# Layer 1's attention: the row scores in one PSUM bank and four parts, the output projection in a bank of its own

## What is computed

```python
def _L1_xattn_ref(values, keys, query, Wv, Wk, Wq, Wo, bo):
    ...                                     # 16 heads of 16 numbers each
    v = jnp.einsum('nlhd,ed->nlhe', v, Wv)
    k = jnp.einsum('nlhd,ed->nlhe', k, Wk)
    q = jnp.einsum('nlhd,ed->nlhe', q, Wq)
    energy = jnp.einsum('nqhd,nkhd->nhqk', q, k)
    attention = jax.nn.softmax(energy / jnp.sqrt(jnp.float32(EMBED)), axis=-1)
    out = jnp.einsum('nhql,nlhd->nqhd', attention, v).reshape(N, Lq, EMBED)
    return out @ Wo.T + bo
...
x = x + _L1_xattn_ref(ctx_1024, ctx_1024, _layernorm(x, axis=-1), ...)
```

## Time and profile before

| what | value |
|---|---|
| median of 3 runs (lowest, highest) | 1107.93 us (1105.76, 1111.91) |
| the profiled execution: its own time, its span | 1103.02 us, 1101.2 us |
| mean granted TensorE clock, of full speed | 0.921 |
| PE busy | 918.6 us, 83% of the span |
| DVE busy | 640.5 us, 58% |
| ACT busy | 490.3 us, 45% |
| POOL busy | 417.8 us, 38% |

### The profile page before, as it was taken

One profiled execution on the slowest core, in us unless ns is written; L12 is line 12 of the kernel. 1 busy time (PEld: TensorE's weight loads), 2 busy tenths in 40 slices (PEclk: granted clock), 3 DMA queues, 4 the chain that ended last, 5 costly groups with the idle time before them and its releaser, 6 DMA issues. The chain is left out here.

```text
span 1101.2 us, 24348 instructions
## 1 busy us (share of the span) xinstructions
PE 918.6 (83%) x8038; PEld 630.3 (57%) x8038; DVE 640.5 (58%) x1554; ACT 490.3 (45%) x832; POOL 417.8 (38%) x560
## 2 busy tenths in 40 slices
PE   6789999997412999999999999997378888877996
PEld 4445555553202888889888988875124444443552
DVE  4556777774697444545444444443698888435561
ACT  1487777775222333333333333322055555634653
POOL 2476776761100334242312222110875553004440
PEclk9799999998655999999999999999589999996998
DMA  6332434331523111111112121111632221000122
GB/s 178 65 105 61 118 97 122 94 105 61 176 83 115 35 54 45 54 47 51 53 45 58 40 58 40 49 31 32 172 92 73 71 66 34 1 1 1 47 51 58
DMA packets 76289, 75.45 MB, mean 69 GB/s; under 512 B 25290, under 2 KB 69434, under 8 KB 76186
## 3 DMA queue, kind: packets, MB, share of 16 engines
q1 hardware_dynamic: 69706, 56.31, 17.6%
q0 software_dynamic: 6480, 17.70, 6.1%
HBM read 51.64 MB, written 22.34 MB: 67 GB/s over the span
## 5 line engine op out<-in xcount | busy, mean ns | idle before, releaser
L1327 DVE CAST hh_e<-h_e 128x512 f16<-128x512 f32 (+1 forms) x156 | 66.7, 427 | 213.2 <-ACT h_e L1303 123.4
L1253 PE MATMUL up_ps<-xT_e,experts 128*128 128x256 f16 (+1 forms) x624 | 165.1, 266 | 4.8 <-ACT h_e L1303 3.2
L1255 PE MATMUL up_ps<-xT_e,experts 128*128 128x256 f16 (+1 forms) x624 | 165.1, 265 | 0.0
L1254 PE MATMUL up_ps<-xT_e,experts 128*128 128x256 f16 (+1 forms) x624 | 164.3, 264 | 0.0
L1267 PE MATMUL y_ps<-experts,hh_e 128*128 x568 | 155.1, 273 | 1.2 <-DVE hh_e L1329 0.3
L1268 PE MATMUL y_ps<-experts,hh_e 128*128 x568 | 155.1, 273 | 0.0
L1269 PE MATMUL y_ps<-experts,hh_e 128*128 x568 | 154.9, 273 | 0.0
L1188 POOL COPY idx_e<-token 128x2 int32 (+2 forms) x39 | 22.5, 577 | 304.6 <-PE xT_ps_e L1233 249.6
L1303 ACT ACTIVATE h_e<-up_ps 128x512 f32<-128x512 f32 (+1 forms) x156 | 87.2, 559 | 109.1 <-PE up_ps L1255 109.1
L1329 DVE TENSOR_TENSOR hh_e<-h_e,hh_e 128x512 f16<-128x512 f32 (+1 forms) x156 | 100.6, 645 | 5.4
L1537 ACT ACTIVATE prob_a<-sT_ps_a 77x1024 f32<-77x1024 f32 x64 | 64.8, 1014 | 50.4 <-PE sT_ps_a L1467 50.4
(11 more groups left out here) (275 smaller groups left out, 1938.0 us busy)
## 6 DMA issues: line engine op xcount, KB each, us to landing
experts<-in_L_ffn_w SPq DMA_DIRECT2D x22, 512.0 KB, 4.1
y_scratch<-y_e SPq DMA_DIRECT2D x32, 256.0 KB, 3.0
w_r<-in_L_ffn_w SPq DMA_DIRECT2D x10, 512.0 KB, 3.8
x<-in_x SPq DMA_DIRECT2D x32, 128.0 KB, 4.1
experts<-in_x SPq DMA_DIRECT2D x64, 64.0 KB, 2.4
x_scratch<-experts SPq DMA_DIRECT2D x16, 256.0 KB, 2.5
xh_scratch<-experts SPq DMA_DIRECT2D x16, 256.0 KB, 2.7
x_a<-x_scratch SPq DMA_DIRECT2D x32, 128.0 KB, 2.1
```

What stands on the lines that cost most here:

```text
L1253: mm(out, w[0], xT[0][:, c, 0:W_], start=c == 0, stop=False)
L1254: mm(out, w[0], xT[1][:, c, 0:W_], start=False, stop=False)
L1255: last = mm(out, w[1], xT[0][:, c, 0:W_], start=False, stop=c == DC - 1)
L1327: nc.vector.tensor_copy(hh[0][own], h[own]).then_inc(hhi_ok, 1)
```

## The change

Two PSUM banks change their use. pair_ps is given up: t_ps and pr_ps each get a bank of their own, and s_ps shrinks from two banks to one. The four score parts are issued one at a time, spread over the step, and each waits for the maxima of the part just ahead of it. The maxima are spread over DVE's list in the same manner. rows_transposed waits for oT_ok (ACT has copied this step's heads out of t_ps) in place of x3_ok; the wait for x3_ok moves from heads_transposed to projection. No instruction of computation is added or taken away.

```diff
-        pair_ps, v_ps = L.bank("pair_ps_a"), L.bank("v_ps_a")
+        t_bank, pr_bank, v_ps, s_ps = (L.bank(f"{n}_ps_a") for n in ("t", "pr", "v", "s"))
...
-        t_ps, pr_ps = pair_ps[:, 0:D], pair_ps[:, D:2 * D]
-        s_ps = ctx.enter_context(nc.psum_tensor("s_ps_a", [P, 2, 512], F32))
+        t_ps, pr_ps = t_bank[:, 0:D], pr_bank[:, 0:D]
...
-                def scores(f, c):
+                def scores(f, i):
+
                     b = f // TB
-                    if c == 0:
+                    if i == 0:
                         pe.wait_ge(hi_ok, f + 1)
-                    for i in range(2):
-                        after(pe, max_ok, 4 * f + 2 * c + i - 1)
-                        mm(s_ps[:, i, 0:CH], xhi[:, f // 4 % 3, c, flat(f % 4, P)],
-                           G["khi"][1][:, b, ds((8 * c + 4 * i) * KEYS, CH)], start=True, stop=True).then_inc(s_done, 1)
+                    after(pe, max_ok, 4 * f + i)
+                    mm(s_ps[:, 0:CH], xhi[:, f // 4 % 3, i // 2, flat(f % 4, P)],
+                       G["khi"][1][:, b, ds(4 * i * KEYS, CH)], start=True, stop=True).then_inc(s_done, 1)
...
                 def heads_transposed(n):
                     pe.wait_ge(o_ok, n + 1)
                     pe.wait_ge(lo_ok, min(n + 11, NT))
-                    after(pe, x3_ok, n)
...
                 def projection(n):
                     pe.wait_ge(oT_ok, n + 1)
+                    after(pe, x3_ok, n)
...
                 def rows_transposed(f):
                     pe.wait_ge(xh_ok, f + 1)
                     after(pe, lo_ok, f)
-                    after(pe, x3_ok, min(f - 10, NT))
+                    after(pe, oT_ok, min(f - 10, NT))
...
                         scores(f, 0)
                     if 0 <= k < QUARTERS:
                         scores_by_key(k)
+                    if tile(f):
+                        scores(f, 1)
                     if tile(n):
                         heads_transposed(n)
                     if 0 <= k - 1 < QUARTERS:
                         values(k - 1)
                     if tile(f):
-                        scores(f, 1)
+                        scores(f, 2)
                     if tile(n):
                         projection(n)
                     if tile(f + 1):
                         rows_transposed(f + 1)
+                    if tile(f):
+                        scores(f, 3)
...
-                def maximum(f, c):
-                    for i in range(2):
-                        dve.wait_ge(s_done, 4 * f + 2 * c + i + 1)
...
+                def maximum(f, i):
+                    dve.wait_ge(s_done, 4 * f + i + 1)
...
                         maximum(f, 0)
                     if tile(f + 1):
                         normed_rows(f + 1)
+                    if tile(f):
+                        maximum(f, 1)
                     if tile(f + 2):
                         rows(f + 2)
+                    if tile(f):
+                        maximum(f, 2)
                     if tile(n):
                         result(n)
                     if tile(f):
-                        maximum(f, 1)
+                        maximum(f, 3)
```

More of the change, by code:

```diff
@@ L1601, in low @@
                                             ALU.subtract).then_inc(lo_ok, 1)
-                def maximum(f, c):
-                    for i in range(2):
-                        dve.wait_ge(s_done, 4 * f + 2 * c + i + 1)
-                        nc.vector.tensor_reduce(nmax[:, f // 4 % 2, f % 4, c, flat(i, 4)],
-                                                s_ps[:, i, 0:CH].rearrange("p (j k) -> p j k", j=4),
-                                                AX.X, ALU.max, negate=True).then_inc(max_ok, 1)
+                def maximum(f, i):
+                    dve.wait_ge(s_done, 4 * f + i + 1)
+                    nc.vector.tensor_reduce(nmax[:, f // 4 % 2, f % 4, i // 2, flat(i % 2, 4)],
+                                            s_ps[:, 0:CH].rearrange("p (j k) -> p j k", j=4),
+                                            AX.X, ALU.max, negate=True).then_inc(max_ok, 1)
                 def maxima(g):
```

## The result

| | median of the runs (lowest, highest) | runs |
|---|---|---|
| before | 1108.53 us (1105.76, 1111.91) | 6 |
| after | 1114.86 us (1113.18, 1116.92) | 6 |

The ratio after to before is 1.0052, with a 95% interval of 1.0032 to 1.0072: the change makes the kernel 6.3 us slower. The prediction said 1113.8 us, slower by 5.9.

A forecast was written before the change was run, and what follows sets the result against it. DVE was taken to bound rows alone, a chain between DVE, PE and ACT rows and quarters, one ring's waits the steady steps. Terms 5.7 + 5.1 - 5.2 + 0.3 = +5.9 us on 1107.93 gave 1113.8 us; range 1108 to 1119.

The forecast's parts named there:

- steps 0 to 4: Five steps with rows and quarters: a ring through PE's list makes 27.15 us against 22.05, +5.1; bounds +1 and +10.
- the base of before: Starting time: the profiled execution's 1103.02 us lies 4.9 below the median, so the forecast adds to 1107.93 us.
- Rows alone: First five tiles, DVE-bound: single-bank stalls before maxima 1, 3 and 0 add 5.7 us; bounds nothing and 6.4.
- 6.35 + 4 x 5.2 = 27.15: Rows-and-quarters regime: first step 6.35 us at the low clock, the other four 5.2 each at full clock.
- rival 1: Clock stays low longer in the rows-and-quarters steps: +1.2 for one more, +5 for all four; 1115 to 1119 us; chance 0.15.
- Steps with all three: Steady 21 tiles: ordinary step 5.22 us against 5.51, sum 115.6 against 120.81, -5.2; bounds 0 and -11.
- the ring: Steady step's last waits: projection, result, new rows' transposes, ACT's copy, DVE's low; PE idles 0.61 for result.
- The end: Step 26: heads_out of the next tile now stands behind scores 3, costing 0.3 us.
- Rival 2: Steady steps don't gain, from longer handoffs or stalls adding up in PE's list: +11, 1119 us; chance 0.12.
- Rival 3: Early steps cheaper: early terms +5 to +8, total 0 to +3, 1108 to 1111 us; chance 0.18.
- Rival 4: Faster: POOL's gathers pace the early regime, stalls fall in slack; -5 to -6, 1102 to 1103 us; chance 0.05.

The follow-up runs named there:

- lend_10: Kernel after, with odd score parts of tiles 0 to 9 in the projection's idle bank: 1103.64 us, ratio 0.9942 to before.
- filler: Kernel after plus useless 512-column matmuls in PE's gaps in steps -5 to 4: 1107.08 us, ratio 0.9977 to before.
- after_again: The kernel after, unchanged, run and profiled once more: 1114.9 us, ratio 1.0042 to before.
- before_filler: Kernel before plus four useless matmuls in each step with rows alone (steps -5 to -1): 1108.61 us, ratio 0.9991 to before.
- pairs: Kernel after's banks, but score parts and maxima in pairs again and result behind the last maximum: 1158.57 us, one execution.
- order_only: Kernel after's spread order of score parts and maxima, on the banks and waits of before: 1117.04 us, ratio 1.0077 to before.
- the second execution: The kernel before, unchanged, profiled once more: that execution took 1112.43 us where the first had 1103.02.
- split: lend_10 with rows divided in two on DVE's list, so xa stands in front of maximum 1: 1096.16 us, ratio 0.9912 to before.
- lend_filler: lend_10 plus four useless matmuls in each step with rows alone (steps -5 to -1): 1103.13 us, ratio 0.9941 to before.

## Why the prediction was right

The median lies 1.1 us above the forecast; the sign was right, and two terms of the sum were right by their steps. The term of steps 0 to 4 left out most of the low clock, and the base of before hid that.

*Rows alone*: +5.7 expected, +5.5 and +5.4 measured. The expected stalls were 0.295, 0.615 and 0.375 before maxima 1, 3 and 0; the idle times are 0.21, 0.53 and 0.27, and idle time counts from the end of the instruction ahead, which overlaps the next by some 0.08. lend_10 takes them away by a second bank and gets 5.0 back.

*Steps 0 to 4*: +5.1 expected, +10.3 and +8.9 measured against the profile that the prediction had. The first is just above the upper bound of +10. The failed step is the sum "6.35 + 4 x 5.2 = 27.15", which let one of five steps be at the low clock. The full-clock price was 0.2 a step too small (filler, 26.99 against 26.0). The steps of the kernel after took 6.59, 6.60, 6.53, 6.00 and 6.64, with a clock of 0.72 in the third, 0.54 in the fourth and 0.50 in the others; in after_again 6.46, 6.60, 6.53, 5.97 and 5.37, with 0.76, 0.50, 0.73, 0.71 and 0.93. This is rival 1's mechanism at its price of about +5, given a chance of 0.15. Between executions of the nearest clocks the term comes out at 4.6 to 4.9, so the banks' part of it was about right. The cause of the low clock is shown only so far that more matmuls in these steps raise it; the same code of before was itself granted 0.91, 0.83 and 0.73. lend_10 has its second bank in these steps too and still took 28.11 us at 0.70, 6 us more than the first execution of before and 1.7 more than before_filler at 0.73: most of that goes with the clock, and why it falls there is open.

*Steps with all three*: 115.6 us expected, 116.32 and 116.88 measured; the steps 5.22, 5.55, 6.12 and 5.0 are 5.27, 5.49, 6.17 and 4.87, and the first is 5.79 and 6.33, before the clock is up. The argument for a gain, that spread parts cover most of the round trip and that result leaves the ring, holds: pairs (1.55 a step without the spreading) and order_only (8.3 or 5.6 lost without the split bank) show that both are needed. The Trainium skill's rule of rotating banks (Perfetto Trace Analysis, Matmuls) speaks rightly in the first regime (5.0 us back in lend_10). In this one the change breaks it for the score parts and follows it for the transposes and the projection, which now have a bank each, and the second weighs more.

*The end*: +0.3 expected. From low(31) to the last result it took 43.2 us in both executions of before and 42.9 in both of after, so it is -0.3.

*The base.* The prediction moved its profiled time to the median by adding 4.9 to the whole, as if what the other executions take more lay where the change doesn't reach. Of the 9.4 us between the two profiled executions of before, 4.2 lie ahead of the attention, but 2.9 in its steps 0 to 4 and 2.7 in its steady part; before_filler, with the same steady code, has 26.38 and 124.15. There the change takes more away: the steady part gains 7.2 and 6.6 against the second execution, where 5.2 was expected, and steps 0 to 4 lose 7.4 and 6.0. Against the first execution nothing cancels, and the sum is 11.3. That the medians differ by 6.3 and 5.9 therefore rests on how a typical execution of before behaves in a ring without slack, which the prediction didn't know of. To that extent the closeness of the number was luck; the median alone would have passed for a full confirmation.

Rival 2 is out, as the steady part gains. Rival 3 is out, as the early steps cost more and not less. Rival 4 is out: POOL is busy 17.50 of 26.23 us, and DVE's idle time ends with PE's scores.

## What to carry to other kernels

A PSUM bank that is written anew after each read costs a round trip of about 0.4 us at full clock and 0.5 at the low one, where nothing else stands between two reads. One instruction of 0.4 us of the reader's list between them left a stall of some 0.15 us at full clock and 0.3 at the low one; two, in split at full clock, left none. Before giving a bank away, ask in which stretches its new owner is idle: lending it back there turned a loss of 0.4 to 0.5% into a gain of 0.6%, and a second small move on DVE's list made it 0.9%. Profile the kernel before more than once where a prediction rests on a few us of a ring: its executions differed by 5.6 us in this part.

## What was not expected of the hardware

The granted clock of one and the same code differs between executions: 0.91, 0.83 and (before_filler) 0.73 in steps 0 to 4 of before, 0.55 and 0.72 of after. With PE busy 4.85 of 5 us (840 to 845 of the kernel after) the clock was still at its 1.2 GHz level. In before_filler and lend_filler a mean clock of 0.75 and 0.66 in the stretch ahead, which had fallen to 0.50 at its end, didn't lead to a higher one behind it.
